# First attention layer of a four-part graph network: per-head sums and exponential unit in another order

## The reference

```
def gatv2(x, edge_index, Wl, bl, Wr, br, att, bias, H, C, concat):
    xl = (x @ Wl.T + bl).reshape(n, H, C)
    xr = (x @ Wr.T + br).reshape(n, H, C)
    s = leaky_relu(xl[src] + xr[dst], 0.2)
    e = einsum('ehc,hc->eh', s, att)
    m = segment_max(e, dst);  p = exp(e - m[dst]);  z = segment_sum(p, dst)
    alpha = p / (z[dst] + 1e-16)
    out = segment_sum(xl[src] * alpha[:, :, None], dst)
    return out.reshape(n, H * C) + bias          # second layer: mean over its one head
h = gatv2(x, edge_index, Wl1, bl1, Wr1, br1, att1, bias1, 4, 32, True)
h = elu(h)
out = gatv2(h, edge_index, Wl2, bl2, Wr2, br2, att2, bias2, 1, 64, False)
```

## Time and profile before

| what | before |
| --- | --- |
| median of 3 runs | 6364.63 us (6355.12 to 6367.59) |
| profiled execution | 6354.62 us, of which the trace's span is 6352.9 us |
| busy in the span | PE 3817.5 us, PEld 2604.5, DVE 4159.4, ACT 2294.0, POOL 4278.3 |
| phase `sum1`, from its barrier to the next | about 4590 to 5040 us of the span |
| busy in 4597 to 5040 (443 us) | DVE 411.1 us, PE 297.8, ACT 146.1, POOL 0 |

### The profile page before, as it was taken

One profiled execution on the slowest core, in us unless ns is written; L12 is line 12 of the kernel. 1 busy time (PEld: TensorE's weight loads), 2 busy tenths in 40 slices (PEclk: granted clock), 3 DMA queues, 4 the chain that ended last, 5 costly groups with the idle time before them and its releaser, 6 DMA issues. The chain is left out here.

```text
span 6352.9 us, 77087 instructions
## 1 busy us (share of the span) xinstructions
PE 3817.5 (60%) x19708; PEld 2604.5 (41%) x19708; DVE 4159.4 (65%) x13369; ACT 2294.0 (36%) x6083; POOL 4278.3 (67%) x4026
## 2 busy tenths in 40 slices
PE   3777788888288878866763444566466557760000
PEld 1444455555155545544543444455355423330000
DVE  6999799999544444434443665666599767765443
ACT  0000477777311111113334555222233279980000
POOL 5777777777677767767775775777300188884777
PEclk9999899999555555555555555788666689985555
DMA  1111344333233333334542454233244445552221
GB/s 40 50 47 47 120 158 158 115 112 100 70 101 106 89 94 97 97 94 128 152 139 81 147 151 132 92 93 94 70 162 173 154 116 141 150 126 78 88 87 63
DMA packets 413613, 684.98 MB, mean 108 GB/s; under 512 B 283685, under 2 KB 290444, under 8 KB 407978
## 3 DMA queue, kind: packets, MB, share of 16 engines
q1 hardware_dynamic: 282410, 542.14, 24.0%
q0 software_dynamic: 130944, 140.05, 11.1%
HBM read 310.94 MB, written 373.78 MB: 108 GB/s over the span
## 5 line engine op out<-in xcount | busy, mean ns | idle before, releaser
L711 POOL DMA_INDIRECT G<-states,srcq x1568 | 1608.5, 1026 | 488.5 <-issue 476.5
L1807 PE MATMUL PS<-ident,HH 128*128 128x128 f32 x2357 | 543.2, 380 | 936.5 <-ACT AT L2076 279.9
L1346 DVE SCALAR_TENSOR_TENSOR R<-R,same,G 128x64 f32<-128x64 f32 x1568 | 447.7, 286 | 829.0 <-DMA G<-states,srcq 645.3
L1807 PEld LDWEIGHTS PS<-ident,HH 128*128 128x128 f32 x2357 | 383.2, 197 | 1044.9 <-issue 481.9
L2076 ACT COPY AT<-PS 128x512 f32<-128x512 f32 (+1 forms) x494 | 283.7, 580 | 1047.6 <-PE PS L1822 719.4
L1822 PEld LDWEIGHTS PS<-WD,AT 128*128 128x128 f32 x2358 | 498.1, 312 | 178.9 <-issue 178.5
L824 POOL DMA_INDIRECT out_nodes<-O,dstq x392 | 432.2, 1103 | 187.5 <-issue 123.3
L1822 PE MATMUL PS<-WD,AT 128*128 128x64 f32 x2358 | 552.6, 412 | 0.0
L711 POOL DMA_INDIRECT EE<-node_info,srcq x392 | 412.5, 1052 | 134.4 <-issue 134.4
L711 POOL DMA_INDIRECT G<-states,srci x392 | 417.3, 1064 | 119.4 <-issue 118.8
L711 POOL DMA_INDIRECT PG<-in_x,dsti x392 | 406.6, 1037 | 119.4 <-issue 118.5
(11 more groups left out here) (413 smaller groups left out, 10053.8 us busy)
## 6 DMA issues: line engine op xcount, KB each, us to landing
states<-O SPq DMA_DIRECT2D x70, 896.0 KB, 3.8
HH<-states SPq DMA_DIRECT2D x56, 896.0 KB
total<-R SPq DMA_DIRECT2D x56, 896.0 KB, 3.7
XB<-resid SPq DMA_DIRECT2D x42, 896.0 KB, 6.1
states<-HH SPq DMA_DIRECT2D x28, 896.0 KB, 5.0
G<-states,srcq POOLq DMA_INDIRECT x1568, 2.5
resid<-XB SPq DMA_DIRECT2D x28, 896.0 KB, 6.8
xl_of_src<-O SPq DMA_DIRECT2D x14, 1792.0 KB, 6.9
```

The lines of the kernel that those rows point to most:

```text
L711: return pool.indirect_dma_start(to, None, table_, bass.IndirectOffsetOnAxis(ap=idx, axis=0), bounds_check=bound, oob_is_err=False).then_i ...
L1346: row = dve.scalar_tensor_tensor(out=R[:, b, j * D:(j + 1) * D], in0=row_before, scalar=same[:, bass.ds(i * C + j, 1)], in1=G[:, b, j * D: ...
L1807: last = pe.transpose(PS[:, 4 + k, q * P:(q + 1) * P], HH[:, b, (g * G4 + q) * D2:(g * G4 + q + 1) * D2], ident[:])
```

## The change

The sums are made edge by edge and group by group. `group_sums(i, b, g)` multiplies four edges by `Ea` in place (L1522 of the changed kernel), makes four running-sum rows of 128 features one after the other (L1525: `row = row_before * same + product`, each waits for the one ahead of it), and multiplies the four rows by `Ec` into `HH` (L1529). Nothing is turned, so that the flags, the scans and `XC`, `SQ` fall away. After each group's sums one `elu` call of two groups before (SUM_LAG) follows.

The exponential unit is written `elu(y) + 1 = relu(y) + min(exp(y), 1)`. ACT makes both parts, `AT = relu(PS + bias1)` (L2185) and `SX = exp(PS + bias1)` (L2186); DVE adds them in one instruction (L1535). The surplus one goes through `WG2` as its column sums, which `prep` subtracts from the bias row `BG2` and from `bias2b`. ACT writes `AT` now, and so waits with `relu` for the products of the group two before; PE's and ACT's loops run over the 98 groups without a seam at the chunk's end, and PE's waits for one group's rows in place of a whole chunk's. PE's program of this phase is written out in full where it was a loop of 7 passes.

The diff, cut to its core:

```
-            def weighted(i, b, between=None):
...
-                for h in range(2):
-                    step(tt(turned_of(PARTS[h]), halves_of(XL[b], h), per_head(Ea, h), ALU.mult))
-                    if i:
-                        step(dve.scalar_tensor_tensor(out=PARTS[h][:, :, 0], in0=FEATS[:, h * D:(h + 1) * D, C - 1], scalar=same[:, i * C:i * C + 1],
-                                                      in1=PARTS[h][:, :, 0], op0=ALU.mult, op1=ALU.add))
...
-                    last = dve.tensor_tensor_scan(out=R[:, 0, h * HC:(h + 1) * HC], data0=FLAGS[i % 2].rearrange("p f t -> p (f t)"),
-                                                  data1=PARTS[h].rearrange("p f t -> p (f t)"), initial=0.0, op0=ALU.mult, op1=ALU.add)
...
-                    last = tt(halves_of(HH[:, b, :], h), turned_of(FEATS[:, h * D:(h + 1) * D, :]), per_head(Ec, h), ALU.mult)
...
-                step(ts(SX[:, k, 0:n * P], SX[:, k, 0:n * P], 1.0, -1.0, ALU.min, ALU.add))
-                dve.wait_ge(s_mult, before["sum1", "group"] + GROUPS * i + g + 1)
-                dve.scalar_tensor_tensor(out=AT[:, k, 0:n * P], in0=PS[:, 4 + k, 0:n * P], scalar=bias1c[:], in1=SX[:, k, 0:n * P],
-                                         op0=ALU.add, op1=ALU.max).then_inc(s_elu, 1)
...
+            def group_sums(i, b, g):
+                if g == 0:
+                    step.reset()
+                    dve.wait_ge(s_ld[b], before["sum1", "ld"] + 16 * (i // 2 + 1))
+                    if i >= 2:
+                        dve.wait_ge(s_st[b], before["sum1", "st"] + 16 * (i // 2))
+                at, first = slice(g * G4 * D2, (g + 1) * G4 * D2), i * C + g * G4
+                step(tt(head_rows(XL[b][:, at]), head_rows(XL[b][:, at]), per_head(Ea, first), ALU.mult))
+                for j in range(g * G4, (g + 1) * G4):
+                    row_before = R[:, b, (j - 1) * D2:j * D2] if j else R[:, 1 - b, (C - 1) * D2:]
+                    step(dve.scalar_tensor_tensor(out=R[:, b, j * D2:(j + 1) * D2], in0=row_before, scalar=same[:, i * C + j:i * C + j + 1],
+                                                        in1=XL[b][:, j * D2:(j + 1) * D2], op0=ALU.mult, op1=ALU.add))
+                if g == GROUPS - 1:
+                    dve.nop().then_inc(s_scan, 1)
+                tt(head_rows(HH[:, b, at]), head_rows(R[:, b, at]), per_head(Ec, first), ALU.mult).then_inc(s_ready, 1)
+
+            def elu(n, k, width=G4):
+                dve.wait_ge(s_exp, n + 1)
+                some = slice(0, width * P)
+                dve.scalar_tensor_tensor(out=AT[:, k, some], in0=SX[:, k, some], scalar=1.0, in1=AT[:, k, some],
+                                         op0=ALU.min, op1=ALU.add).then_inc(s_elu, 1)
...
+            for n in range(ALL + SUM_LAG):
+                if n < ALL:
+                    group_sums(n // GROUPS, n // GROUPS % 2, n % GROUPS)
+                if n >= SUM_LAG:
+                    elu(n - SUM_LAG, (n - SUM_LAG) % 2)
...
+            for n in range(ALL + 2):                                    # PE
+                if n < ALL:
+                    if n >= 2 and n % GROUPS < 2:
+                        pe.wait_ge(s_elu, n - 1 + AHEAD)
+                    turn("sum1", n // GROUPS, n // GROUPS % 2, n % GROUPS, freed=ready)
+                if n >= 2:
+                    multiply("sum1", (n - 2) // GROUPS, (n - 2) // GROUPS % 2, (n - 2) % GROUPS, *how, ready=ready)
...
                 act.wait_ge(s_elu, GROUPS * i + g + 1)
+                act.wait_ge(s_mult, before[phase, "group"] + GROUPS * i + g + 1)
+                act.activation(AT[:, k, 0:n * P], PS[:, 4 + k, 0:n * P], ACT.Relu, bias=bias1c[:])
                 act.activation(SX[:, k, 0:n * P], PS[:, 4 + k, 0:n * P], ACT.Exp, bias=bias1c[:]).then_inc(s_exp, 1)
...
-                act.copy(FLAGS[i % 2][:, :, 1:], same[:, i * C + 1:(i + 1) * C].unsqueeze(1).broadcast_to([P, D, C - 1])).then_inc(s_flags, 1)
...
+            step(tt(bias2b[:], bias2b[:], PS[:, 3, D:2 * D], ALU.subtract))       # prep
+            step(tt(BG2[:, D:], BG2[:, D:], PS[0:1, 3, D:2 * D], ALU.subtract))
+            step(tt(BG2[:, D:], BG2[:, D:], PS[0:1, 3, 2 * D:3 * D], ALU.subtract))
...
+            pe.matmul(PS[:, 3, D:3 * D], cols[:, MISS:MISS + 1].broadcast_to([P, P]), WG2[:], start=True, stop=True).then_inc(s_carry, 1)
```

More of the change, by code:

```diff
@@ L348, in build_program @@
         plan("att1", ld=TURNS * 16, st=TURNS * 16, gath=TURNS * 16 * G4, ready=CHUNKS, group=GROUPS * CHUNKS, patch=16)
-        plan("sum1", ld=TURNS * 16, st=TURNS * 16, scan=CHUNKS, ready=CHUNKS + 1, group=GROUPS * CHUNKS + 1, carry=1,
+        plan("sum1", ld=TURNS * 16, st=TURNS * 16, scan=CHUNKS, ready=ALL + 1, group=GROUPS * CHUNKS + 1, carry=1,
              patch=16, patched=32)
@@ L624, in sums @@
                     load_sums(i + 2, b)
-                sp.wait_ge(s_ready, before["sum1", "ready"] + 1 + i)
+                sp.wait_ge(s_ready, before["sum1", "ready"] + GROUPS * (i + 1))
                 sp.dma_start(chunk(total_g1, i, 2 * CD), HH[:, b, :]).then_inc(s_st[b], 16)
@@ L1550, in elus @@
-            def elus(i, b):
-                def some(groups):
-                    for g in groups:
-                        elu(i, b, g)
-                return some
-            dve.sem_inc(s_elu, AHEAD)
-            for k in range(2):
-                step(dve.memset(FLAGS[k], 0.0))
-            dve.nop().then_inc(s_flags, 1)
-            weighted(0, 0)
-            for i in range(1, CHUNKS):
-                weighted(i, i % 2, elus(i - 1, (i - 1) % 2))
-            for g in range(GROUPS):
-                elu(CHUNKS - 1, 1, g)
+            def group_sums(i, b, g):
[13 more added lines that the diff above has]
+                tt(head_rows(HH[:, b, at]), head_rows(R[:, b, at]), per_head(Ec, first), ALU.mult).then_inc(s_ready, 1)
@@ L1791, in _ @@
             pe.wait_ge(s_prep, 3)
-            pe.matmul(PS[:, 3, 0:D], cols[:, SCR:SCR + 1].broadcast_to([P, P]), WG2[:, 0:D], start=True, stop=True).then_inc(s_carry, 1)
+            pe.matmul(PS[:, 3, 0:D], cols[:, SCR:SCR + 1].broadcast_to([P, P]), WG2[:, 0:D], start=True, stop=True)
+            pe.matmul(PS[:, 3, D:3 * D], cols[:, MISS:MISS + 1].broadcast_to([P, P]), WG2[:], start=True, stop=True).then_inc(s_carry, 1)
             barrier()
             def turn(phase, i, b, g, n=G4, freed=None):
-                if phase in LAYERS:
+                if phase in LAYERS or phase == "sum1":
                     pe.wait_ge(s_ready, before[phase, "ready"] + GROUPS * i + g + 1)
@@ L1937, in _ @@
             ready = lambda i, g: (s_elu, GROUPS * i + g + 1 + AHEAD)
-            paired(pe, TURNS, products("sum1", *how, ready=ready))
+            for n in range(ALL + 2):
[5 more added lines that the diff above has]
+                    multiply("sum1", (n - 2) // GROUPS, (n - 2) // GROUPS % 2, (n - 2) % GROUPS, *how, ready=ready)
             barrier()
-            pe.matmul(PS[:, 3, 0:D2], CARRY[:], FEATS[:, :, C - 1], start=True, stop=True).then_inc(s_carry, 1)
+            pe.matmul(PS[:, 3, 0:D2], CARRY[:], R[:, 1, (C - 1) * D2:], start=True, stop=True).then_inc(s_carry, 1)
             turn("sum1", CHUNKS, 0, 0, 1)
@@ L2210, in _ @@
                 act.sem_inc(s_rows[b], 32)
[L2212 to L2230 removed]
+            for n in range(ALL + 2):
+                if n < ALL:
+                    exponential("sum1", n // GROUPS, n // GROUPS % 2, n % GROUPS)
+                if n >= 2:
+                    second_operands("sum1", (n - 2) // GROUPS, (n - 2) // GROUPS % 2, (n - 2) % GROUPS, it=(n - 2) // GROUPS // 2)
             barrier()
```

58 lines of the change are left out of this document (9 added, 49 removed).

## The result

| | before | after |
| --- | --- | --- |
| median | 6366.11 us of 4 runs (6355.12 to 6373.02) | 6268.12 us of 4 runs (6265.33 to 6271.1) |
| ratio | | 0.9848, 95% interval 0.9831 to 0.9865 |
| profiled execution | 6354.62 us (span 6352.9) | 6269.06 us (span 6267.4) |
| `sum1`, first multiply to last copy | 442.6 us | 348.7 us |

Forecast were 6273 us and 91.6 us less; measured are 6268 us and 98 us less between the medians.

The account below looks back on a forecast made before the run. DVE was taken to set the pace in `sum1`: 93.1 us less there, minus 1.5 more in `prep`, gave 91.6 us less. From the median 6364.63 that made 6273 us, range 6245 to 6318.

Parts of the forecast that it names:

- The group: DVE in `sum1`: two multiplies, four dependent rows and one addition cost 3.49 us a group.
- The row: One running-sum row of 128 columns on DVE: 0.352 us, 0.387 with L1453's hop of 0.035; the layers' hop is 0.14.
- a chunk's head: Resetting the step counter and the `nop` that frees the load add perhaps 0.1 us in each chunk, 1.4 in all.
- The phase: `sum1` from first multiply to last copy: last copy at 4946.5 where it was 5039.58, 93.1 us less.
- `prep`: Stands on the path: a second matmul of 0.7 us and three subtractions of 0.25 each cost 1.5 us more.
- ACT and the load: In `sum1`, ACT's 2.0 us out of 3.49 a group is covered by DVE; no wait for the next load.
- PE and the ring: The DVE, PE, ACT loop over two groups takes 6.2 us at PE's lower clock against DVE's 7.0: does not bind.
- (a): Rival: PE stays at the lower clock and bounds `sum1` at 3.90 us a group, 40 us more, 6313 us; chance 0.13.
- (b): Rival: the multiplies keep their old price because heads' factors, not turning, cost; 78 us more, 6351 us; chance 0.10.
- (c): Rival: the ring goes round once for each group, not for two; 265 us more, 6538 us; chance 0.05.
- The part on DVE: In a `sum1` chunk: sums 8.4 to 10.8 us, multiplies 13.6 to 9.3, unit 8.1 to 4.3; seven groups 24.5 against 29.74.
- busy over 95% of the phase: Sign to look for in the changed trace: DVE busy over 95% of a `sum1` phase of some 350 us.

Follow-up runs that it names:

- experiment 4: The changed kernel with two more activations per group on ACT, results unread, between relu and exponential: 6275.9 us, 8 us more than the changed kernel.
- experiments 5: The changed kernel with five unread DVE instructions of 1792 columns behind the phase, to price head factors and turning: a single run, 6279.3 us.
- experiment 9: Experiment 8 with twelve transposes, results unread, at each chunk's head on PE: 6326.4 us, ratio 0.9941.
- experiment 8: The kernel before with the new exponential unit, its units placed later, none behind a chunk's first `Ea` multiply: 6353.5 us, ratio 0.9976.

## Why the prediction was right, point by point

- **The group.** 3.49 us were forecast, from prices of other lines; 3.48 is what the timeline has. The row was right at 352 ns, with L1453's hop and not the layers'. At a chunk's head the distance is 3.60, so 0.12 us for the step counter and the `nop`, where 0.1 stood as an estimate.
- **The phase.** 4597.0 to 4946.5 was forecast, 349.5 us; it took 4602.94 to 4951.66, 348.7. Up to the end of the unit of group 95 that was 342.7 against 341.8, and behind it 6.8 against 6.9. A sixth of the gain (16.3 of 93.9 us) came at the end, since in the old order most of the last chunk's units ran after the last sums.
- **`prep`.** 1.5 us were forecast. From the start of the minimum to the start of the copy it took 1.20 us before and 2.59 after, 1.4 us more:

```profile
1712.86 0.66 PE L1771 MATMUL PS<-WG,cols 128*128 128x64 f32 x2 [77.36 <-DVE cols L1278]
1713.31 0.74 PE L1772 MATMUL PS<-WG,cols 128*128 128x128 f32 x2
1714.09 0.22 DVE L1280 TENSOR_TENSOR bias2b<-bias2b,PS 128x64 f32<-128x64 f32 x1 [1.38 <-PE PS L1772]
```

  The first of these stood at 1707.99 before: 4.7 us of the difference arose ahead of `prep`, in code that the change does not touch. Another 2.4 us arose behind `sum1`. So the profiled executions differ by 85.6 us and not by 92.5 (93.9 less 1.4). The medians differ by 98; the runs of the kernel before spread over 18 us, so that the forecast's 6273 came within 5 us of 6268 partly by luck. The phase itself, 349.5 against 348.7, did not.
- **ACT and the load** stayed hidden, as forecast: ACT has 1.2 us of room in a group (experiment 4), and DVE waits for a load only at the phase's start. The 0.69 us of one activation is not in the earlier trace rows, which has 1.28 for two; the changed trace has it (0.687).
- **PE and the ring.** The statement was that the ring has 0.8 us to spare at the lower clock. It has: in the spells at 0.50 DVE runs on at its pace. One group of such a spell:

```profile
4733.44 0.69 DVE L1529 TENSOR_TENSOR HH<-R,EE 128x512 f32<-128x512 f32 x1
4734.05 0.69 DVE L1535 SCALAR_TENSOR_TENSOR AT<-SX,AT 128x512 f32<-128x512 f32 x1
...
4734.74 0.69 ACT L2185 ACTIVATE AT<-PS,bias1c 128x512 f32<-128x512 f32 x1 [2.82 <-DVE AT L1535]
4734.88 1.09 PE L1787 MATMUL PS<-ident,HH 128*128 128x128 f32 x4 [0.26 <-DVE AT L1535]
...
4736.92 0.69 DVE L1529 TENSOR_TENSOR HH<-R,EE 128x512 f32<-128x512 f32 x1
```

  PE's transposes take 1.09 us there and its gap has shrunk to 0.26; DVE's distance is still 3.48. PE falls behind by 3.90 - 3.48 = 0.42 us a group, closes its gaps, and in these two spells the clock came back before the slack was used up.
- **The rivals.** (a) did not happen: in the spells PE lost its gaps and came back to the higher clock, which is the reason given against it. But that work without a gap brings the clock back is no rule. In experiment 9 it stayed at 0.50 through 20 us of it, so that the forecast was less safe against (a) than its text has it. Something like (a) is what the slow chunks of experiment 8 show, where PE at the lower clock and its gap fill the 30.7 us. (b) and (c) fell with experiments 5 and 4.
- **What was wrong.** The part on DVE adds the unit's saving to the sums' as if each were there by itself ("the unit from 8.1 to 4.3 us" in a chunk). The total of the sum came out, but the terms don't add: alone the unit brought 0 and not some 50 us. The sum held because the new order spaces the groups evenly, a condition that the text did not name as part of the price. One sign was missed too: DVE was to be busy over 95% of the phase and was 93%, since the idle time ahead of its dependent instructions (7.0 us ahead of the rows of `XB`, 5.0 ahead of the `Ec` multiplies) counts as idle.

## What to carry to other kernels

An engine's shorter instructions can be worth nothing if the other engine in the ring doesn't get its work at even distances: a unit some 50 us shorter brought nothing in one order and 44 us in another, and the same instructions in pairs took 29 us more. Before moving work, look for the place in a period where PE stands idle longest; filling that gap gave back 27 us here. Layouts that turned an operand on DVE cost 70% more here than ones that didn't (3.42 against 2.03 us), with or without a broadcast factor, and the factor applied to every row could be folded into one that is applied anyway, for 69 us.

## What the runs showed that was not expected

- Useless matmuls made a kernel faster: twelve transposes a chunk, 6353.5 to 6326.4 us, with PE's clock up from 0.63 to 0.76.
- One program has two rhythms in one execution: chunks of 27.1 us at 0.75 to 0.81 and of 30.7 at 0.56, most of them followed by others of their kind (experiment 8).
- In the changed kernel, at an even rhythm, PE went down to 0.50 and up again several times in each of two spells (4710 to 4760 and 4850 to 4900 us), with DVE unmoved.
- PE at 0.50 for 20 us without a gap in its work (experiment 9).
- Beside POOL's multiplies four of DVE's rows took 4.40 us and not 1.51.
